# First attention of a transformer block on one core: ScalarE writes minus the row maxima into the score banks, the products add onto them, and the side work is spread over the steps

## What is computed

```python
# first attention: 16 heads of 64
xn = layernorm(x)
q, k, v = split(xn @ W_qkv + b_qkv); k = k + pos_enc
x = x + softmax(q @ k.T / 8) @ v @ W_out + b_out
# then the block of `ffn`: 16 heads of 8, router, 4 experts of width 512
xn = layernorm(x)
a  = softmax(q2 @ k2.T * 8**-0.5) @ v2 @ Wo + bo
z  = layernorm(xn + a) * g1 + c1
e  = floor(z @ router_w + router_b) mod 4
x  = x + layernorm(z + sum_e where(expert == e, relu(z @ W1[e] + b1[e]) @ W2[e] + b2[e], 0)) * g2 + c2
```

## Time and profile before

| What | Value |
|---|---|
| Time, median of 3 runs | 2300.61 us (2297.51 to 2304.11) |
| Time of the profiled execution | 2298.73 us |
| Its span, first to last instruction | 2296.9 us |
| PE busy | 2195.3 us, 96% |
| DVE busy | 1765.2 us, 77% |
| POOL busy | 1236.5 us, 54% |
| ACT busy | 1209.8 us, 53% |
| Mean granted TensorE clock | 0.974 |
| First attention, from the first `fin` to the last | 69.5 to 1401.6 us |

### The profile page before, as it was taken

How to read it: one execution, slowest core, us unless ns; L and a number is a source line. 1 busy time by engine, 2 the same in 40 slices (tenths; PEclk the granted TensorE clock), 3 DMA queues, 4 the chain that set the end, 5 groups by cost and what they waited for, 6 DMA issues and landing times.

```text
span 2296.9 us, 36401 instructions
## 1 busy us (share of the span) xinstructions
PE 2195.3 (96%) x13030; PEld 1056.8 (46%) x13030; DVE 1765.2 (77%) x2826; ACT 1209.8 (53%) x1781; POOL 1236.5 (54%) x763
## 2 busy tenths in 40 slices
PE   5999999999999999999999999899999999999997
PEld 2545555555555555555555544333333333333334
DVE  5686787787787787787787775779999999999913
ACT  0334444444444444444444435258888878888882
POOL 1587687687687687687687668542004015005103
PEclk8899999999999999999999999869999999999998
DMA  3000000000000000000000000000000000000000
GB/s 116 1 1 1 1 1 1 1 1 1 1 1 1 1 1 1 1 1 1 1 1 1 1 19 1 1 1 2 1 1 1 2 1 6 2 2 6 1 1 10
DMA packets 12269, 11.33 MB, mean 5 GB/s; under 512 B 2112, under 2 KB 10944, under 8 KB 11968
## 3 DMA queue, kind: packets, MB, share of 16 engines
q1 hardware_dynamic: 12096, 9.01, 1.3%
HBM read 7.69 MB, written 1.05 MB: 4 GB/s over the span
## 4 chain that ended last, share of the span: by engine, by line
PE 68%; DVE 15%; issue 9%; POOL 5%; ACT 2%; DMA 0%; SPq 0%; DVEq 0%; POOLq 0%; ACTq 0%
PE acc_o L487 14%; PE scores L470 10%; PE acc_o L606 10%; PE scores L592 9%; PE ring L450 5%; DVE accp L1306 5%; DVE mxp L1378 4%; POOL accp L935 3%; DVE mxp L1272 3%; PE scores L475 3%; ACT prob L800 2%; PE ring L651 2%; PE ring L659 2%; PE ring L572 2%; PE ring L414 2%
## 5 line engine op out<-in xcount | busy, mean ns | idle before, releaser
L785 ACT ACTIVATE prob<-scores 128x1024 f32<-128x1024 f32 x512 | 525.2, 1026 | 614.6 <-PE scores L475 572.8
L935 POOL TENSOR_TENSOR accp<-accp,prob 128x1024 f32<-128x1024 f32 x318 | 782.0, 2459 | 93.1 <-ACT prob L785 62.3
L1272 DVE TENSOR_REDUCE mxp<-ring 128x1 f32<-128x512 f32 x1024 | 637.3, 682 | 208.3 <-PE ring L450 208.1
L800 ACT ACTIVATE prob<-scores 128x512 f32<-128x512 f32 x1024 | 543.5, 599 | 139.4 <-PE scores L592 137.7
L1378 DVE TENSOR_REDUCE mxp<-ring 128x1 f32<-128x512 f32 x789 | 509.7, 683 | 54.5 <-PE ring L572 39.4
L487 PE MATMUL acc_o<-prob,v 128*64 128x512 f32 x2048 | 498.6, 608 | 0.0
L470 PE MATMUL scores<-q_all,k_all 64*128 64x512 f32 x3072 | 473.9, 409 | 0.0
L470 PEld LDWEIGHTS scores<-q_all,k_all 64*128 64x128 f32 x3072 | 275.2, 185 | 179.9 <-issue 129.3
L592 PE MATMUL scores<-q_all,k_all 32*128 32x512 f32 x1024 | 307.2, 494 | 13.4 <-ACT prob L800 8.7
L450 PE MATMUL ring<-k_all,q_all 64*128 64x512 f32 x1024 | 283.9, 429 | 33.8 <-DVE mxp L1272 28.8
L572 PE MATMUL ring<-k_all,q_all 32*128 32x512 f32 x789 | 285.0, 503 | 10.0 <-DVE mxp L1378 5.2
(11 more groups left out here) (185 smaller groups left out, 1682.5 us busy)
## 6 DMA issues: line engine op xcount, KB each, us to landing
w_all<-w_pairs SPq DMA_DIRECT2D x1, 1344.0 KB, 10.1
pos_sb<-pos SPq DMA_DIRECT2D x1, 1024.0 KB, 5.7
w_sb<-w SPq DMA_DIRECT2D x4, 256.0 KB, 4.5
mrow<-m_rows SPq DMA_DIRECT2D x64, 2.0 KB
w_all<-w SPq DMA_DIRECT2D x1, 1024.0 KB, 5.3
q_all<-m_rows SPq DMA_DIRECT2D x64, 2.0 KB
...
```

Source lines behind the costliest of these rows:

```text
L785: nc.scalar.activation(prob[:, T % SLOTS1, :, :], sc[T % 2][:, :, :], ACT.Exp, scale=SCALE1).then_inc(exp_done, 1)
L800: nc.scalar.activation(prob2[:, h // 2, T % 2, h % 2, :], sc2[place % 3], ACT.Exp, scale=SCALE2).then_inc(exp2_done, 1)
L935: nc.gpsimd.tensor_tensor(accp[:, k % 2], accp[:, k % 2], prob[:, T % SLOTS1], ALU.add).then_inc(pool_acc, 1)
L1272: done(nc.vector.reduce_max(mxp1[k % 2][:, h * QT + q, kc:kc + 1], bank[:], AX.X), ("max", k, q, kc, h))
```

## The change

- **Seeds.** For T > 1 the two matmuls of L475 are gone. ACT writes a tile `minus_all` (minus the maxima, the same row in all 128 partitions, both heads) into both banks of `sc[T % 2]` with a Copy of 128 x 1024, right after the exp of the tile before in the same banks (`seed`). PE's products start with start=False and so add onto it. `scores(T)` waits for the seed and not for the exp.
- **minus.** `minus_all` is made once for each chunk: an item `minus` after step 5 multiplies `onesw` with `mrow` into two banks of the ring, and ACT copies them to SBUF (`minus_copy`). `fin` moves from step 5 to step 4, and DVE's last reduction over the maxima (`mred`) from step 5 to step 4.
- **Side tiles apart.** The four maxima tiles of a step are no longer issued in two pairs behind each `scores`, but one ahead of the first `scores`, two ahead of the second, one behind it (`sides1`; a helper `max1` issues one tile).
- **Adds apart.** DVE's four adds stand one each at steps 6, 7, 0 and 1, behind the maxima of the step.
- **Normalising.** POOL normalises after its last add (tile 11), not after tile 9.
- **Queries.** The rounded part of Q is written by ACT (`rounded_queries`), no longer by DVE.
- **Start.** Eight couples of chunk 1 stand ahead of the loop in place of six.
- **Second attention.** The projection `Q2` stands at step 3 of a block, not 4.

```diff
@@ -54,7 +54,7 @@
 
 
 COUPLES = [(q, kc) for kc in range(NC) for q in range(QT)]
-EARLY1 = 6
+EARLY1 = 8
 
 
 def last_item1(k, j):
@@ -67,8 +67,10 @@
     if j in (3, 6) and k // NC + 1 < PAIRS:
         half = 0 if j == 3 else 1
         return ("K", k // NC + 1, 2 * c + half) if c < 2 else ("V", k // NC + 1, 2 * (c - 2) + half)
+    if j == 4 and k + 1 < CHUNKS1:
+        return ("fin", k + 1)
     if j == 5 and k + 1 < CHUNKS1:
-        return ("fin", k + 1)
+        return ("minus", k + 1)
     if j == (7 if k < LAST1 else 4) and k > 0:
         return ("y", k - 1)
     return None
...
@@ -103,6 +105,11 @@
     return tiles[2 * n:2 * n + 2]
 
 
+def seeded1(T):
+
+    return T > 1
+
+
 def couple1(k, j, half):
 
...
@@ -113,12 +120,23 @@
     return (to, *COUPLES[n]) if to < CHUNKS1 else None
 
 
+def sides1(k, j):
+
+    tiles = []
+    for half in range(2):
+        cp = couple1(k, j, half)
+        if cp:
+            tiles += [("max", *cp, h) for h in range(2)]
+        tiles += tiles_late1(k, j, half)
+    return tiles[:1], tiles[1:3], tiles[3:]
+
+
 def start1():
     tiles = [[("couple", 0, q, kc) for q in range(QT)] for kc in range(NC)]
     early = [("couple", 1, *c) for c in COUPLES[:EARLY1]]
     return ([("T", c) for c in range(NC)] + [("Q", 0), ("K", 0, 0), ("V", 0, 0), ("V", 0, 1), ("K", 0, 1)] + tiles[0]
             + [("K", 0, 2)] + tiles[1] + [("K", 0, 3), ("V", 0, 2), ("V", 0, 3)] + tiles[2] + [("Q", 1)] + tiles[3]
-            + [("rows",)] + early[:3] + [("fin", 0)] + early[3:])
+            + [("rows",)] + early[:3] + [("fin", 0)] + early[3:] + [("minus", 0)])
 
 
...
@@ -189,7 +206,7 @@
             items.append(("K2", n + 2, (5, 7, 8, 9).index(t)))
     if t == 1 and n > 0:
         items.append(("o", n - 1))
-    if t == 4 and n + 2 < BLOCKS2:
+    if t == (3 if n > 0 else 4) and n + 2 < BLOCKS2:
         items.append(("Q2", n + 2))
     if t == MAX2_STEPS and n + 1 < BLOCKS2:
         items.append(("fin2", n + 1))
...
@@ -460,20 +481,35 @@
                 k, t = T // NT, T % NT
                 p, c, u = k // NC, k % NC, T % 2
                 of_keys = slice(t * 128, (t + 1) * 128)
-                if T >= 2:
+                if seeded1(T):
+                    pe.wait_ge(seeded, T - 1)
+                elif T >= 2:
                     pe.wait_ge(exp_done, T - 1)
                 if t == 0:
                     wait_free(pe, ("Q", k))
                     pe.wait_ge(kl_ready, NC * (p + 1))
                 for n, (of_k, of_q) in enumerate(((khi, qhi), (khi, qlo), (klo, qhi))):
                     for h in range(2):
-                        nc.tensor.matmul(sc[u][:, h, :], of_k[half(h), p % 2, of_keys], of_q[half(h), c, :],
-                                         start=(n == 0), stop=False)
-                if t == 0:
+                        last = nc.tensor.matmul(sc[u][:, h, :], of_k[half(h), p % 2, of_keys], of_q[half(h), c, :],
+                                                start=(n == 0 and not seeded1(T)), stop=(n == 2 and seeded1(T)),
+                                                skip_group_check=seeded1(T))
+                        if n == 2 and seeded1(T):
+                            last.then_inc(sc_ready[u], 1)
+                if seeded1(T):
+                    return
+                if t < 2:
                     pe.wait_ge(m_dma, 32 * (k + 1))
                 for h in range(2):
                     nc.tensor.matmul(sc[u][:, h, :], onesw[half(h), :], mrow[half(h), k % 2, :],
                                      start=False, stop=True).then_inc(sc_ready[u], 1)
+
+            def minus(k):
+
+                pe.wait_ge(m_dma, 32 * (k + 1))
+                for h in range(2):
+                    bank = begin(("minus", k, h))
+                    end(nc.tensor.matmul(bank[:], onesw[half(h), :], mrow[half(h), k % 2, :], start=True, stop=True),
+                        ("minus", k, h))
 
             def values(T):
                 k, t = T // NT, T % NT
...
+                    scores(0)
+                    scores(1)
                 item1(it)
-            pe.wait_ge(blank, 4)
-            scores(0)
-            scores(1)
             for k in range(CHUNKS1):
                 for j in range(STEPS1):
-                    for n in range(2):
+                    for n, tiles in enumerate(sides1(k, j)):
+                        for it in tiles:
+                            if it[0] == "max":
+                                max1(*it[1:])
+                            else:
+                                item2(it)
                         T = NT * k + 2 * (j + 1) + n
-                        if T < NT * CHUNKS1:
+                        if n < 2 and T < NT * CHUNKS1:
                             scores(T)
-                        cp = couple1(k, j, n)
-                        if cp:
-                            couple(*cp)
-                        for it in tiles_late1(k, j, n):
-                            item2(it)
                     values(NT * k + 2 * j)
                     values(NT * k + 2 * j + 1).then_inc(pv_done, 1)
                     it = last_item1(k, j)
...
@@ -767,6 +806,12 @@
                 nc.scalar.activation(v1[:, p % 2, b * QT:(b + 1) * QT, :], ring[bank_of(("V", p, b))][:]
                                      .rearrange("p (t n) -> p t n", t=QT), ACT.Copy).then_inc(free[bank_of(("V", p, b))], 1)
 
+            def rounded_queries(k):
+                p, c = k // NC, k % NC
+                wait_full(act, ("Q", k))
+                nc.scalar.activation(qhi[:, c, :], ring[bank_of(("Q", k))][:], ACT.Identity,
+                                     bias=bqk_all[:, p, 0:1]).then_inc(qh_ready, 1)
...
@@ -783,6 +828,22 @@
                     else:
                         act.wait_ge(dve_acc, dve_adds(old))
                 nc.scalar.activation(prob[:, T % SLOTS1, :, :], sc[T % 2][:, :, :], ACT.Exp, scale=SCALE1).then_inc(exp_done, 1)
+
+            def seed(T):
+
+                if T % NT < 4:
+                    for h in range(2):
+                        wait_free(act, ("minus", T // NT, h))
+                act.wait_ge(exp_done, T - 1)
+                nc.scalar.activation(sc[T % 2][:, :, :], minus_all[:], ACT.Copy).then_inc(seeded, 1)
+
+            def minus_copy(k):
+                for h in range(2):
+                    wait_full(act, ("minus", k, h))
+                    if k > 0:
+                        act.wait_ge(seeded, NT * k - 2)
+                    nc.scalar.activation(minus_all[:, h, :], ring[bank_of(("minus", k, h))][:],
+                                         ACT.Copy).then_inc(free[bank_of(("minus", k, h))], 1)
 
...
                                          bias=b1_sb[:, e * FT + f:e * FT + f + 1]).then_inc(free[bank_of(it)], 1)
 
             deviation(1)
+            act.wait_ge(pair0_dma, 16 * 2)
             for it in start1():
                 if it[0] == "V":
                     v_copy(*it[1:])
+                elif it[0] == "Q":
+                    rounded_queries(it[1])
             exps(0)
             exps(1)
+            minus_copy(0)
+            seed(2)
...
@@ -1090,7 +1163,7 @@
                     add(NT * k + t)
                     if t == 1 and k >= CHUNKS1 - 2:
                         deviations(0, k - CHUNKS1 + 2, stats2, rstd_ready)
-                    if t == (9 if k < LAST1 else 6) and k > 0:
+                    if t == (POOL_ADDS if k < LAST1 else 6) and k > 0:
                         normalise(k - 1)
                     if t == 8 and last_item1(k, 3) and last_item1(k, 3)[0] == "K":
                         split_keys(*last_item1(k, 3)[1:])
@@ -1252,10 +1325,8 @@
             def q_proj(k):
                 p, c = k // NC, k % NC
                 bank = open_(("Q", k))
-                bias = bqk_all[:, p, 0:1]
-                nc.vector.tensor_scalar(qhi[:, c, :], bank[:], bias, None, ALU.add).then_inc(qh_ready, 1)
                 dve.wait_ge(qh_ready, k + 1)
-                done(nc.vector.scalar_tensor_tensor(qlo[:, c, :], bank[:], bias, qhi[:, c, :].bitcast(F32),
+                done(nc.vector.scalar_tensor_tensor(qlo[:, c, :], bank[:], bqk_all[:, p, 0:1], qhi[:, c, :].bitcast(F32),
                                                     ALU.add, ALU.subtract), ("Q", k))
 
...
@@ -1562,18 +1633,18 @@
 
             for k in range(CHUNKS1):
                 for j in range(STEPS1):
-                    if j == STEPS1 - 3 and k + 1 < CHUNKS1:
+                    if j == STEPS1 - 4 and k + 1 < CHUNKS1:
                         mred(k + 1)
                     for n in range(2):
                         cp = couple1(k, j, n)
-                        if j == 0 and k > 0:
-                            add(NT * k - 2 + n)
-                        elif j == STEPS1 - 1 and k < LAST1:
-                            add(NT * k + NT - 4 + n)
                         if cp:
                             couple(*cp)
                         for it in tiles_late1(k, j, n):
                             item2(it)
```

(4 more changed lines are left out.)

33 lines of the change are left out of this document (23 added, 10 removed).

## The result

| | before | after |
|---|---|---|
| Time, median | 2301.58 us (4 runs) | 2247.64 us (4 runs, 2247.04 to 2248.8) |
| Ratio, 95% interval | | 0.9768 [0.9751, 0.9785] |
| Span of the profiled execution | 2296.9 us | 2245.2 us |
| PE, DVE busy | 2195.3, 1765.2 us | 2099.1, 1741.8 us |
| ACT, POOL busy | 1209.8, 1236.5 us | 1757.7, 1226.4 us |

A forecast was written before the change was run, and what follows sets the result against it. PE's queue was taken as the bound: steps, items, `minus` and waits sum to a 41.5 us chunk against 42.97, -45.6 over 31 chunks; with start and end -44, so 2256 us, range 2218 to 2308.

The forecast's parts named there:

- PE's step: One loop step on PE without waits: from 4.51 to 4.11 us, or 4.22 if the scores' extra 0.11 stays.
- A bit under half of what the removed matmuls promise is lost: PE's step: of the 0.46 us of removed L475 pairs, a bit under half goes to maxima tiles issued alone.
- `minus`: 0.25 predicted: On PE after step 5: one more pair of matmuls, 0.25 us in a chunk, with no wait for DMAs.
- Waits: PE's waits in a chunk: 1.0 after `minus`, 0.8 after `Q`, 0.1 after K, 0.5 in step 1, 0.5 for `sums`.
- After `minus`: Step 6: PE waits 1.0 us for the second ring bank, as ACT's copies come behind two exps and two seeds.
- after `Q`: PE's third maxima tile waits 0.8 us for its ring bank, held by ACT's and then DVE's part of Q.
- Step 1: PE waits 0.5 us for its first maxima tile's bank, wanted at 5.97 after step 0 starts, free at 6.46.
- ACT just follows, with nothing to spare: Steps without an item: second seed ends at 5.23 us, the next second scores want it at 5.24; no wait.
- DVE's adds: DVE's add waits for POOL's running add: about 2.7 us in step 0, under 1.5 in step 1.
- POOL keeps its turn: Rival, step 1: DVE misses a 0.04 us margin, POOL's next add runs first, `sums` waits 2.4 us longer; 2330 us, chance 0.13.
- The rest: Outside the per-chunk gain: +3.9 us ahead of the loop, -0.9 in chunk 30, -1.5 in chunk 31, 0 for `Q2`.
- The waits at step 7 of before go: DVE's adds at steps 6 and 7 meet an idle POOL, so the kernel before's waits at step 7 vanish.

The follow-up runs named there:

- e1: The changed kernel with the maxima tiles in pairs again, one pair behind each scores: 2251.21 us, ratio 0.978.
- e7: The changed kernel with late-bank maxima tiles behind the second scores (step 6 all three, steps 3, 4 and 7 the third): 2228.46 us, ratio 0.9691.
- e12: The kernel before with DVE's adds one to a step and POOL normalising last, nothing else: 2328.38 us, ratio 1.0138.
- e2: The changed kernel with DVE's four adds back in place, two at step 7 and two at step 0, ahead of their maxima: 2293.58 us, ratio 0.9970.

## Why the prediction was right, and where not

The forecast was a chunk of 41.5, 1.47 less than before. By the means I used, the chunk went from 42.97 to 41.29, 1.68 less; by the median distances from 43.0 to 41.5, 1.5 less. The chunk came out as forecast, but through two mis-sized terms of opposite direction, which is in part luck.

- **PE's step: 4.11 predicted, 3.91 measured.** I let the lone first tile cost 0.21, less the 0.11 that I took from the scores; together they cost 0.02. For the lone last tile I had 0.43, and it costs 0.31. Over a chunk that is 1.6 us less than forecast. "A bit under half of what the removed matmuls promise is lost" does not even follow from the sum beside it (0.06 of 0.46, or 0.17 with the 0.11 left in), and it is wrong: 0.46 were removed and the step is 0.60 shorter, since a lone last tile is cheaper than a pair.
- **`minus`: 0.25 predicted, 0.34 measured** (569.84 to 570.18).
- **Waits: 2.9 predicted, 41.5 - 8 x 3.91 - 5.45 - 0.34 = 4.4 measured** in the median chunk (4.2 by the mean of 41.29). After `minus` 1.15 (said 1.0), after `Q` 1.08 (0.8), `sums` 0.56 (0.5): right in place and nearly in size. After K 0.17 (0.1; 436.87 to 439.08 from start to values is 2.21), so in all but two of the K steps between 120 and 1300 us; the 0.5 in my expectations for e1 and e7 is that of the two others. In step 1 1.0, not 0.5, and in step 5 0.35, not 0.
- **Step 1** waits for the bank that I named, the one that DVE's reduction frees. I had the reduction in time (bank free 6.46 after the start of step 0, measured 6.51), but PE wants the bank 0.3 earlier, since step 0 is 0.2 shorter and the last tile comes 0.1 sooner in its step. So the error of the first term fed the third.
- **Step 5, "ACT just follows, with nothing to spare."** Seeds of 1.03, a gap of 0.02, 4.09 for four: as forecast. Three other times were off: the step is 0.2 shorter, its second scores want their seed 1.05 into it and not 1.13, and the first exp starts 1.26 into it and not 1.13. Together that is 0.4, against the 0.2 that `fin` left to spare: the second scores start 0.24 late, at 566.85, and take 0.11 longer. The late exp goes with the lone first tile: in e1, which has none, the exp starts 1.03 after its scores (569.03, scores 568.00). So the tile that costs PE 0.02 delays ACT by 0.2.
- **DVE's adds.** 2.73 in step 0 and 1.21 in step 1, as worked out, in nearly all chunks. The rival "POOL keeps its turn" came in one chunk between 120 and 1300 us, at its price: POOL's add was let in at 170.23 (167.53 and 2.70) and ends 2.36 later, at 172.59. DVE, held up by the 0.28 of L1361, came at 172.76, 0.17 too late, and `sums` waited 2.46. So the margin of hundredths was real. In e12 DVE is 0.64 late in every chunk, and the wait is 2.2.
- **The rest: +1.5 predicted for start and end.** The 30 chunks behind the second `fin` (105.7 us before, 107.3 after) gave 1.80 each, 54 us, and the whole span gave 51.7; so all else cost 2.3. My sum has 44 for the same 30 chunks and nothing for all else (1.47 for the one chunk more, against +1.5). Of the ten more, eight are odd chunks of the kernel before and not a better median chunk. The last distance went from 45.9 to 39.8: at 1372.27 the kernel before waits 2.00 for maxima, and its granted clock is then 0.61 up to 1376. That these single waits are gone was no term of mine.
- **"The waits at step 7 of before go"**: e2 bears it out, and puts more weight on it than my sum did. Without the spread adds the rest of the change gains 7 us; without the rest, they lose 32.

The frame of the prediction was right: it counted PE's starts, then each bank, and the places of the waits that it named are those of the trace, but for step 5. What it had no place for is that the parts do not add: by their ratios, L475 removed alone is +22 us, the adds apart alone +32, the whole order alone -30, and all together -54.
